# A selective-scan kernel on one core: the logarithm's passes in three pieces, layer norm products and sums in other places

## The reference, cut to what matters

```python
xp = einsum('bld,ed->ble', x, x_proj_w)            # x is layernorm(input) here
delta = softplus(einsum('blr,dr->bld', xp[..., :64], dt_proj_w) + dt_proj_b)
deltaA = exp(delta * A)                            # 16 states per channel
h = deltaA[t] * h + delta[t] * B[t] * x[t]         # for every t of 1024
y[t] = sum over the 16 states of h * C[t]
x = x + (y + x_norm * D)
# then: (x1 - mean) / sqrt(var + eps) of the rows of x1, router weights, chosen tokens, output
```

## Time and profile before

| | us |
|---|---|
| median of 3 runs | 4587.35 (4586.65 to 4588.29) |
| profiled execution | 4590.48 |
| its span | 4588.0 |
| VectorE busy | 3844.8 (84%) |
| GpSimd busy | 3435.0 (75%) |
| ScalarE busy | 2824.3 (62%) |
| PE busy | 2972.6 (65%) |

### The profile page before, as it was taken

How to read it: one execution, slowest core, us unless ns; L and a number is a source line. 1 busy time by engine, 2 the same in 40 slices (tenths; PEclk the granted TensorE clock), 3 DMA queues, 4 the chain that set the end, 5 groups by cost and what they waited for, 6 DMA issues and landing times. The chain is left out here.

```text
span 4588.0 us, 60367 instructions
## 1 busy us (share of the span) xinstructions
PE 2972.6 (65%) x17062; PEld 1351.1 (29%) x17062; DVE 3844.8 (84%) x3098; ACT 2824.3 (62%) x4359; POOL 3435.0 (75%) x1748
## 2 busy tenths in 40 slices
PE   3656565656575656566665656565654289999997
PEld 1222222222222222222222222222222145555553
DVE  3999999999999999999999999999998645555542
ACT  5777777777767777777777777777665223232221
POOL 3999999999999999999999999999997100000010
PEclk7667575656565656666575657565655599999998
DMA  4454546364645455454545463646443300000000
GB/s 104 97 135 116 151 105 163 82 167 93 161 102 143 114 136 144 106 140 111 139 115 148 103 159 88 166 93 162 101 126 74 147 13 21 18 18 18 18 19 7
DMA packets 198217, 472.87 MB, mean 103 GB/s; under 512 B 60688, under 2 KB 61200, under 8 KB 197088
## 3 DMA queue, kind: packets, MB, share of 16 engines
q1 hardware_dynamic: 177136, 452.11, 38.9%
q0 software_dynamic: 20736, 16.88, 1.4%
HBM read 126.83 MB, written 73.43 MB: 44 GB/s over the span
## 5 line engine op out<-in xcount | busy, mean ns | idle before, releaser
L882 POOL TENSOR_TENSOR ch<-hid,cmat 128x1024 f32<-128x1024 f32 x1024 | 2391.6, 2362 | 120.3 <-DVE hid L751 102.5
L751 DVE TENSOR_TENSOR_SCAN hid<-decay,inp 128x1024 f32<-128x1024 f32 x1024 | 2270.1, 2268 | 122.6 <-ACT decay L604 122.6
L398 PE MATMUL ps_y<-ch,nsum 128*32 128x256 f32 x8192 | 949.9, 564 | 860.9 <-POOL ch L882 859.2
L604 ACT ACTIVATE decay<-delr,a_neg 128x1024 f32<-128x1024 f32 x1024 | 1133.4, 1113 | 562.1 <-DVE hid L751 550.0
L740 DVE TENSOR_TENSOR inp<-dx,bmat 128x1024 f32<-128x1024 f32 x880 | 1012.6, 1208 | 63.1 <-ACT dx L612 63.1
L398 PEld LDWEIGHTS ps_y<-ch,nsum 128*32 128x32 f32 x8192 | 254.6, 141 | 1527.3 <-POOL ch L882 1313.6
L409 PE MATMUL ps_y<-ident,ysb 128*128 128x128 f32 x1024 | 339.7, 431 | 289.2 <-ACT ysb L619 275.7
L409 PEld LDWEIGHTS ps_y<-ident,ysb 128*128 128x128 f32 x1024 | 246.9, 298 | 524.7 <-ACT ysb L619 484.6
L393 PE MATMUL ps_y<-xhT,dskip 128*32 128x256 f32 x2048 | 260.4, 599 | 217.1 <-ACT xr L626 217.1
L1135 POOL DMA_INDIRECT out_rows<-row,idx_out x16 | 41.1, 2571 | 402.4 <-issue 221.3
L847 POOL TENSOR_TENSOR inp<-dxr,bmat 128x1024 f32<-128x1024 f32 x144 | 340.1, 2362 | 0.0
(11 more groups left out here) (167 smaller groups left out, 3952.7 us busy)
## 6 DMA issues: line engine op xcount, KB each, us to landing
dxr<-dxT SPq DMA_DIRECT2D x1024, 128.0 KB, 2.4
delr<-delT SPq DMA_DIRECT2D x1024, 128.0 KB, 2.4
xr<-in_x SPq DMA_DIRECT2D x32, 1024.0 KB, 6.5
bmat<-b_and_c SPq DMA_DIRECT2D x256, 128.0 KB, 3.4
cmat<-b_and_c SPq DMA_DIRECT2D x256, 128.0 KB, 3.0
x_rows<-xr SPq DMA_DIRECT2D x16, 2048.0 KB, 7.6
out_rows<-xr SPq DMA_DIRECT2D x32, 1024.0 KB, 4.6
w<-in_w SPq DMA_DIRECT2D x2, 4096.0 KB, 24.2
```

What stands on the lines that cost most here:

```text
L398: last = pe.matmul(ps_y[q * CH:(q + 1) * CH, 0:2 * P], nsum[:], ch[:, g, q * 2 * P:(q + 1) * 2 * P], start=False, stop=(g == GROUPS - 1))
L604: nc.scalar.activation(decay[:, g % 2, :], delr[:, c % 2, :], ACT.Exp, scale=a_neg[:, i:i + 1])\
L751: nc.vector.tensor_tensor_scan(hid[:, g, :], decay[:, g % 2, :], inp[:, g, :], 0.0, ALU.mult, ALU.add).then_inc(hid_ready, 1)
L882: nc.gpsimd.tensor_tensor(ch[:, g, :], hid[:, g, :], cmat[:, g, :], ALU.mult).then_inc(ch_ready, 1)
```

## The change

The tables and `exp_log` change; no instruction is added or taken away. `exp_log` takes a list of parts: 0 is Exp, 1 is the first Identity and Ln, 2 the last Identity. The table `LOG` places them. For k = 0 all stay at (12, 3). For k = 1 they go from (13, 3) to places 0, 1 and 2 of chunk 14, for k = 2 from (15, 3) to places 0, 1 and 2 of the next batch's chunk 0, for k = 3 from (4, 3) to those of chunk 5. Between part 0 and part 1 ScalarE makes the decays (c,2) and (c,3), between part 1 and part 2 the decay (c+1,0). GpSimd's steps that read them go one or two tiles later. The sums of both layer norms, the output products and GpSimd's end of the second layer norm get other places.

```diff
@@ -36,9 +36,10 @@
 PROJECT = (((10, 0), (10, 0), (10, 1), (10, 1)), ((10, 3), (11, 0), (11, 0), (11, 1)))
 COPY_PROJ = ((10, 3), (11, 3))
 
-SUMS1 = {(5, 2): range(0, 2), (5, 3): range(2, 5), (6, 0): range(5, 8), (6, 1): range(8, 11), (6, 2): range(11, 14), (6, 3): range(14, 17)}
-SUMS2 = {(0, 2): range(0, 3), (0, 3): range(3, 6), (1, 0): range(6, 8), (1, 1): range(8, 11), (1, 2): range(11, 13), (1, 3): range(13, 15), (2, 0): range(15, 17)}
-MAKE_OUT = ((3, 1), (3, 1), (3, 2), (3, 2), (3, 3), (3, 3), (3, 3), (3, 3))
+SUMS1 = {(5, 3): range(0, 3), (6, 0): range(3, 6), (6, 1): range(6, 9), (6, 2): range(9, 13), (6, 3): range(13, 17)}
+SUMS2 = {(0, 2): range(0, 2), (0, 3): range(2, 4), (1, 0): range(4, 6), (1, 1): range(6, 8), (1, 2): range(8, 10),
+         (1, 3): range(10, 12), (2, 0): range(12, 13), (2, 1): range(13, 15), (2, 2): range(15, 17)}
+MAKE_OUT = ((3, 1), (3, 2), (3, 2), (3, 3), (3, 3), (4, 0), (4, 0), (4, 1))
 NORM1 = 7
 
 
@@ -47,14 +48,19 @@
 
 
 DELTA = {(13, 0): (1, 0, 0), (13, 1): (1, 0, 1), (13, 2): (1, 0, 2), (13, 3): (1, 0, 3),
-         (14, 1): (1, 1, 0), (14, 3): (1, 1, 1), (15, 2): (1, 1, 2), (1, 0): (0, 1, 3),
-         (0, 2): (0, 2, 0), (1, 2): (0, 2, 1), (2, 0): (0, 2, 2), (3, 0): (0, 2, 3),
-         (5, 2): (0, 3, 0), (6, 0): (0, 3, 1), (6, 2): (0, 3, 2), (7, 1): (0, 3, 3)}
+         (14, 3): (1, 1, 0), (15, 0): (1, 1, 1), (15, 2): (1, 1, 2), (1, 0): (0, 1, 3),
+         (0, 3): (0, 2, 0), (1, 2): (0, 2, 1), (2, 0): (0, 2, 2), (3, 0): (0, 2, 3),
+         (5, 3): (0, 3, 0), (6, 0): (0, 3, 1), (6, 2): (0, 3, 2), (7, 1): (0, 3, 3)}
+
+
+LOG = {(12, 3): (1, 0, (0, 1, 2)), (14, 0): (1, 1, (0,)), (14, 1): (1, 1, (1,)), (14, 2): (1, 1, (2,)),
+       (0, 0): (0, 2, (0,)), (0, 1): (0, 2, (1,)), (0, 2): (0, 2, (2,)),
+       (5, 0): (0, 3, (0,)), (5, 1): (0, 3, (1,)), (5, 2): (0, 3, (2,))}
 
 RW_COPY = (2, 0)
 ROUTER = (2, 3)
 FINISH1 = (7, 0)
-FINISH2 = (2, 1)
+FINISH2 = (2, 3)
 OWN = GROUPS - 1
 OWN_AT = (3, 5, 6, 8, 9, 10, 11, 12, 13)
 ROUTED = (4, 2)
@@ -513,18 +519,21 @@
                 nc.scalar.activation(dxT[:, k, half], aux[:], ACT.Relu, bias=dtb[:, k:k + 1])\
                     .then_inc(aux_emptied, 1)
 
-            def exp_log(b, k):
+            def exp_log(b, k, parts=(0, 1, 2)):
 
                 n = b * KD * ZACT + k * ZACT
-                act.wait_ge(z_act, n + 2)
-                nc.scalar.activation(te[:], te[:], ACT.Exp, scale=-1.0).then_inc(z_act, 1)
-                if has(b, 1) or k > 0:
-                    act.wait_ge(delta_step, b * KD * 3 + 3 * (k - 1) + 2)
-                act.wait_ge(z_act, n + 3)
-                nc.scalar.activation(tu[:], te[:], ACT.Identity, bias=1.0).then_inc(z_act, 1)
-                nc.scalar.activation(delT[:, k, :], te[:], ACT.Ln, bias=1.0).then_inc(z_act, 1)
-                act.wait_ge(z_act, n + 4)
-                nc.scalar.activation(tu[:], tu[:], ACT.Identity, scale=-1.0, bias=1.0).then_inc(z_act, 1)
+                if 0 in parts:
+                    act.wait_ge(z_act, n + 2)
+                    nc.scalar.activation(te[:], te[:], ACT.Exp, scale=-1.0).then_inc(z_act, 1)
+                if 1 in parts:
+                    if has(b, 1) or k > 0:
+                        act.wait_ge(delta_step, b * KD * 3 + 3 * (k - 1) + 2)
+                    act.wait_ge(z_act, n + 3)
+                    nc.scalar.activation(tu[:], te[:], ACT.Identity, bias=1.0).then_inc(z_act, 1)
+                    nc.scalar.activation(delT[:, k, :], te[:], ACT.Ln, bias=1.0).then_inc(z_act, 1)
+                if 2 in parts:
+                    act.wait_ge(z_act, n + 4)
+                    nc.scalar.activation(tu[:], tu[:], ACT.Identity, scale=-1.0, bias=1.0).then_inc(z_act, 1)
 
             def copy_rw(b, emptied):
 
@@ -662,7 +671,8 @@
                     z_half(b, 3, 0)
                 if c == Z3 and place == 3:
                     z_half(b, 3, 1)
-                    exp_log(b, 3)
+                if at in LOG and not LOG[at][0] and (LOG[at][1] == 3 or has(b, 1)):
+                    exp_log(b, *LOG[at][1:])
                 if has(b, 1):
                     if at in SUMS2:
                         ln2_sums(b - 1, 1 - par, SUMS2[at])
@@ -690,7 +700,8 @@
                     z_half(b + 1, Z.index(c), 0)
                 if c in Z and place == 3:
                     z_half(b + 1, Z.index(c), 1)
-                    exp_log(b + 1, Z.index(c))
+                if at in LOG and LOG[at][0]:
+                    exp_log(b + 1, *LOG[at][1:])
 
             def body(b, par):
                 final = is_last(b)
```

## The result

The changed kernel takes 4564.11 us (median of 5 runs, 4562.58 to 4566.04), before 4587.35; the ratio is 0.9948, 95% interval 0.9938 to 0.9958. That is 23.2 us less. It lies inside the whole stated range (4530 to 4577) but outside the forecast's own (4540 to 4562), 14 us short of the 37.2 us that were forecast and nearer to rival B's 4573 than to 4550.

What follows compares the result with a forecast made beforehand. VectorE bounds the short stretch from (0,2) to (5,2), GpSimd the rest. 22.5 us at (0,3) plus 14.7 at (5,2) make 37.2 us less, giving 4550 us; own range 4540 to 4562, whole range 4530 to 4577.

Steps and rivals of the forecast that it cites:

- rival B: Gain at (0,2) goes into new waits, only the 14.7 us at (5,2) is left: 4573 us; chance 0.14.
- the two stretches: VectorE sets the pace from (0,2) to (5,2), 71.6 us; GpSimd from there to the next (0,2), 144.8 us.
- rival A: VectorE binds throughout, so all 55.1 us of its stalls at (0,2) and (5,2) come back: 4532; chance 0.11.
- the prediction's list: GpSimd's idle times read from its timeline: (0,2) 0.73 and 2.35 us, (4,0) 3.75, (5,2) 1.81 to 0.43.
- The idle time at (4,0): GpSimd's idle time there, 3.75 us before, was to be 2 to 3.7 us after the change.
- the bound at (0,3): Scan of (0,3) waits behind the copy of ps_y and GpSimd's `ch` of (15,3): gain 1.56 us, not 2.01.
- the sums: Six sums in front of the decay of (1,2) just fit; with eight at old places it is 1.0 us late.
- I count 0.3 us of stall there: At (1,2) in jump batches: the copy to xr waits 0.66 us for PE instead of 0.21.
- rival C: Slower: passes moved in front of decay (1,2) make VectorE wait 4.3 us there: 4614; chance 0.06.
- for no gain: k=1 in GpSimd's stretch: `ch` of (14,2) to (15,0) come 2.4 us earlier, VectorE runs further ahead; 0 us.
- k=2 with the sums: Passes moved from (15,3) into chunk 0, gain at (0,3) 22.5 us, ends 0 and 34.4; sums taken as 0.
- k=3: Passes moved from (4,3) into chunk 5; GpSimd's idle time at (5,2) goes, 14.7 us, ends 0 and 20.7.

Runs made afterwards that it cites:

- experiment 7: Changed kernel with all layer norm work (sums, outputs, end of the second layer norm) back at its old places: 4582.17 us, 0.9987.
- experiment 8: Changed kernel with PE's loop over four batches and Identity and Ln of k=2 in front of the copy to xr: 4550.20 us, 0.9917.
- experiment 11: Kernel before with all layer norm work at its new places, every pass and step at its old place: 4587.60 us, 1.0000.
- Experiment 1: Changed kernel with PE's loop alone turning over four batches instead of two: 4553.59 us, 0.9927.
- 2: Changed kernel with Identity and Ln of k=2 put in front of the copy to xr in chunk 0, no longer at (0,1): 4555.28 us, 0.9928.
- 5: Kernel before with PE's loop alone turning over four batches: 4588.77 us, 1.0001.
- 6: Kernel before with the three pieces for k=1 alone and GpSimd's steps behind (14,3) and (15,0): 4568.29 us, 0.9957.
- experiment 9: Kernel before with only GpSimd's two steps for k=1 moved behind (14,3) and (15,0), no pass moved: 4569.95 us, 0.9959.
- experiment 10: Kernel before with pieces and steps for k=1 and k=3; k=2 in one piece, layer norm work at old places: 4553.83 us, 0.9924.
- 12: Changed kernel, but of k=2 only the last Identity goes to (0,2); Exp, Identity and Ln stay at (15,3): 4554.43 us, 0.9926.
- experiment 3: Kernel before with the three pieces for k=3 alone and the step behind (5,3); layer norm work at old places: 4570.84 us, 0.9965.

## Why the prediction was right and where it failed

**Right: the two stretches.** Cut at the same two tiles, the long stretch lasts 145.7 us on average in the kernel before and 145.5 to 145.9 in every other kernel but that of experiment 7 (146.3); only the short one shrank, from 70.7 to 69.2 and in experiment 8 to 68.3. The best kernel gains 37.8 us, far from rival A's 55. Which of GpSimd's idle times would pay was read wrongly, though: the prediction's list leaves out (1,0), where GpSimd's timeline before shows

```profile
958.65 2.35 POOL L882 TENSOR_TENSOR ch<-hid,cmat 128x1024 f32<-128x1024 f32 x1 [1.02 <-DVE hid L751]
```

and 19.2 us over the trace, of which 2.2 are left. The idle time at (4,0), forecast to fall to 2 to 3.7 us, is 3.0 to 4.4 us and has not fallen in sum. The stretch table after answers to the earlier trace rows; its third and fourth rows are the next batch, without a jump:

```profile
730.00:799.70 69.70, 37.58 (x248) 16.48 (x252) 67.38 (x54) 53.65 (x90) 64.10 (x36) 0.55 0.61 173
799.70:944.90 145.20, 93.65 (x597) 38.47 (x597) 140.32 (x83) 106.60 (x157) 144.34 (x68) 0.66 0.47 107
945.00:1013.30 68.30, 36.79 (x244) 15.77 (x240) 68.09 (x54) 52.31 (x88) 63.75 (x35) 0.55 0.61 174
1013.30:1158.80 145.50, 92.98 (x585) 38.48 (x582) 140.35 (x82) 105.19 (x154) 144.64 (x68) 0.63 0.46 108
```

VectorE fills 68.09 of 68.3 us of the short stretch without a jump, but only 67.38 of 69.7 with one; the long one kept its length to 0.7 us and GpSimd its 144.3 to 144.6 us. The Trainium skill's plain rule (Perfetto Trace Analysis, Identifying the Most-Contended Engine) names VectorE, whose gaps rival A priced at 55 us; its remark on regimes (Optimization Strategy, same page) is what the runs bear out.

**Right: the bound at (0,3), and the sums.** Without a jump the scan of (0,3) came 1.1 us late behind the copy of y and nothing was late at (1,2): the interval is the forecast's. Eight sums there cost 1.18 us a batch without a jump against 1.0 (experiment 7), and the moves are worth 0 alone (experiment 11).

**Wrong: the stall in the jump batches, the step "I count 0.3 us of stall there".** VectorE waits 0.9 us at (1,1) and 1.2 us at (1,2), 2.1 us in five of the six and 4.1 us in the sixth, together 14.5 us where the sum had 1.8. That is 12.7 of the 14 us that are missing. I took PE's lateness in those batches from the earlier trace rows, 0.66 us. That was the smallest of the six (0.66 to 1.50), and only what was left of it beneath ScalarE's block. With the block gone `ysb` is ready 1.2 to 1.9 us earlier against `ch` of (15,3), and PE, still in its own jump, starts at most 0.3 us earlier. Experiment 1 shows the place (10.5 us), 2 the mechanism (8.8 us), 5 that it cost nothing before. (The sum counts seven batches with a jump; the trace has six, as the last batch stands behind the loop.) It is rival C's mechanism, the crowd in front of (1,2), in six batches instead of fifteen and at half its price.

**Wrong: k=1, the step "for no gain".** The total hid this. I priced that stretch by GpSimd's idle time. For the passes that fits: moved as well, they bring 19.7 us instead of 18.3, which can't be told from nothing (experiments 6 and 9). But the steps change the order within it: the product of (14,3) comes forward and that of (15,3) does not, so what hangs on the first gains 2.4 us on what hangs on the second, and k=2's block hangs on the first. It was worth 18.3 us alone (experiment 9). It and the split of k=2 work against the same bound at (0,3), so beside each other they don't add, and the split then brings only its crowd: k=1 and k=3 without it are 4553.8 us, with it and the sums 4564.1 (experiment 10 and the changed kernel). The loss is in the batches with a jump; without PE's jump the split costs nothing that shows (experiments 1 and 8). That the split of k=2 costs some 10 us here is the difference of two medians of different comparisons; the size is uncertain by several us, the sign is borne out by 12 as well.

**Luck.** That the total lay within the range owes something to chance. k=1 was put at 0 and brings some 19 us alone; k=2 with the sums was put at 22.5 and brings 8.1 alone and, beside the other two, some -10. The two misses have opposite signs.

**Right, but wide: k=3.** 14.7 forecast, 17.0 measured, the interval holds both.

**Open.** One batch with a jump lost 4.1 us and the others 2.1. The trace shows that PE's gap itself was longer there, where the other five have 2.79 to 3.05:

```profile
2019.80 0.79 PE L415 MATMUL ps_y<-ident,ysb 128*128 128x128 f32 x2 [4.94 <-issue]
```

In 3 us of this gap the profile's DMA view has two packets of instructions, 16 KB each, with 6.8% of the 16 engines' time; in 3 us around each of the other five gaps it has one, with 1.8 to 2.3%. Over all traces the eight gaps of PE at this place above 4 us (4.14 to 4.94) hold two such packets, the 64 shorter ones behind a jump (up to 3.83 us) one each. That PE waits for these loads, and why there are two at times, is not shown. What splits 3's 17.0 us from 14.7 is not settled for the median: its traced execution, the fastest, has some 5 us from the clock, and the slower ones have no trace.

## What to carry to other kernels

When a block in front of a wait is taken away, look at what every other engine does in that same moment, its loop's jump too: a lateness of 0.66 us read beneath a block of 4 us is a lower bound of what the engine behind it needs. In a stretch that another engine sets, more speed was worth nothing here, but another order was: one line that moved two steps of GpSimd behind later tiles brought three quarters of what the whole change did. Test the parts alone even where the total comes out near the forecast; here three parts that bring 8, 17 and 20 us alone bring 23 together, and leaving one out is faster as long as PE's jump is in its way.

The Trainium skill (Perfetto Trace Analysis, Optimizing Scalar/DVE Operations) says that breaking up instructions of an engine that isn't saturated may let others finish sooner. Here a run of four passes was broken up, and no single instruction. Of that it held at k=3 (17.0 us); at k=2, where the pieces landed in the stretch that counts, it brought 8.1 us alone and nothing beside the others.

## What the runs showed of the hardware

- In front of PE's first product behind a loop's jump the changed kernel shows 2.79 to 3.05 us of issue and once 4.94; without a jump PE idles 0.50 us in the same place. Behind its input PE starts 2.25 to 2.52 us late and once 4.41, against 0.05 without a jump. ScalarE's jump shows 0.76 to 1.78 us of issue in the two kernels. The price of PE's jump in the time is 0 where nothing waits for it (experiment 5) and 2.3 us where the next instruction is waited for (216.3 against 214.0, experiment 1).
- The releaser named for a gap is the one that came last: the same gap of PE in front of batch 3 is put down to "ACT ysb" before and to "issue" after, and PE's turn starts 6.2 and 6.3 us behind `ch` of (15,3).
- The same product of PE took 2.07 us at a granted clock of 0.50 and 1.12 us at 0.89 to 1.00. At the lower level ScalarE waits 0.65 us for it, and in batches 4 to 14 without a jump VectorE's stall at (0,2) is 2.0 us (kernel before) instead of 1.3 (experiment 3).
- The eight longest gaps of PE behind a jump, 4.14 to 4.94 us, hold two 16 KB packets of the instruction queue, the 64 shorter ones (up to 3.83 us) one.
